# Routing tokens to experts for the second time: a shorter choice, roots between the scatters, and places and ranks in another order

## The reference

```python
x = _layernorm(x + attn(x))                      # softmax(q k^T) per batch, then v and Wo
x = _layernorm(x + expert_mlp(x, token_ids))     # expert = token_id // 3125, weights from ctx
x = _layernorm(x + ffn(x))                       # router, top 1 of 4 experts
# expert_mlp: silu(x Wg[e]^T) * (x Wu[e]^T), then Wd[e]^T; the weights are ctx_2048 (256 x 256 per expert)
# ffn: logits = x @ Wr + br; probs = softmax(logits); e = argmax; out = probs[e] * (silu(x Wg[e]) * (x Wu[e])) @ Wd[e]
```

## Time and profile before

| | us |
|---|---|
| runs, median of 3 | 197.58 (197.44 to 198.25) |
| span of the profiled execution | 194.3 |
| median above the span | 3.3 |
| PE busy | 176.0 (91%) |
| DVE, ACT, POOL busy | 132.0, 103.3, 103.0 |

### The profile page before, as it was taken

One profiled execution on the slowest core, in us unless ns is written; L12 is line 12 of the kernel. 1 busy time (PEld: TensorE's weight loads), 2 busy tenths in 40 slices (PEclk: granted clock), 3 DMA queues, 4 the chain that ended last, 5 costly groups with the idle time before them and its releaser, 6 DMA issues.

```text
span 194.3 us, 3905 instructions
## 1 busy us (share of the span) xinstructions
PE 176.0 (91%) x969; PEld 140.0 (72%) x969; DVE 132.0 (68%) x406; ACT 103.3 (53%) x274; POOL 103.0 (53%) x130
## 2 busy tenths in 40 slices
PE   1999997999999898989999999999999999999810
PEld 0677775447888655668888788888888888888610
DVE  3269996895678887536554454444799986888950
ACT  3136776725567935537664946643665422455530
POOL 7006356770126884627772168860588810377683
PEclk9999999999999999999999999999999999999975
DMA  5999999246999223146544105444050000011010
GB/s 157 359 336 418 378 366 319 73 139 168 322 334 405 101 85 94 29 130 173 221 149 150 46 0 165 164 162 167 0 162 3 0 0 3 0 57 56 22 62 24
DMA packets 15317, 29.14 MB, mean 150 GB/s; under 512 B 1726, under 2 KB 11968, under 8 KB 15170
## 3 DMA queue, kind: packets, MB, share of 16 engines
q1 hardware_dynamic: 13568, 25.68, 39.4%
q0 software_dynamic: 1440, 3.22, 4.7%
q10 hardware_dynamic: 290, 0.01, 0.1%
HBM read 20.41 MB, written 9.28 MB: 153 GB/s over the span
## 4 chain that ended last, share of the span: by engine, by line
PE 68%; POOL 11%; issue 7%; DMA 5%; DVE 3%; ACT 3%; POOLq 1%; SPq 1%; DVEq 0%; ACTq 0%
PE bank L484 14%; PE bank L486 13%; PE bank L485 13%; POOL out_tokens L473 5%; PE bank L729 4%; PE bank L563 4%; PE bank L652 3%; PE bank L629 3%; POOL rstd L395 3%; DMA arena<-in_attn_w 3%; PE bank L594 2%; PE bank L572 2%; PE bank L511 2%; DMA x_sorted<-buf,slot 1%; PE bank L498 1%
## 5 line engine op out<-in xcount | busy, mean ns | idle before, releaser
L391 POOL TENSOR_TENSOR w_lo<-stage,w_hi 128x512 fp32r<-128x512 f32 x40 | 51.4, 1305 | 44.0 <-ACT w_hi L803 44.0
L912 ACT ACTIVATE gate<-bank 128x256 f32<-128x256 f32 x44 | 17.0, 387 | 48.5 <-PE bank L486 48.5
L1206 DVE TENSOR_TENSOR hid<-bank,gate 128x256 f32<-128x256 f32 x44 | 18.7, 425 | 30.5 <-ACT gate L912 30.2
L484 PE MATMUL bank<-w_hi,xr 128*128 x88 | 35.9, 408 | 1.4 <-DVE xr L1164 0.8
L486 PE MATMUL bank<-w_hi,xr 128*128 x88 | 34.7, 395 | 0.0
L485 PE MATMUL bank<-w_lo,xr 128*128 x88 | 34.7, 394 | 0.0
L484 PE MATMUL bank<-w_hi,hT 128*128 x88 | 28.5, 324 | 0.7 <-DVE hT L1211 0.7
L803 ACT ACTIVATE w_hi<-stage 128x512 fp32r<-128x512 f32 x48 | 28.6, 630 | 0.3 <-PE bank L486 0.3
L486 PE MATMUL bank<-w_hi,hT 128*128 x88 | 24.9, 282 | 0.0
L485 PE MATMUL bank<-w_lo,hT 128*128 x88 | 24.8, 282 | 0.0
L484 PEld LDWEIGHTS bank<-w_hi,xr 128*128 128x128 f32 x88 | 16.6, 189 | 4.4 <-issue 2.3
(11 more groups left out here) (182 smaller groups left out, 329.7 us busy)
## 6 DMA issues: line engine op xcount, KB each, us to landing
stage<-in_w_ffn SPq DMA_DIRECT2D x16, 768.0 KB, 4.5
rows<-x_sorted SPq DMA_DIRECT2D x22, 132.0 KB, 2.3
x_sorted<-padrow SPq DMA_DIRECT2D x1, 2244.0 KB, 10.2
x_sorted<-padrow SPq DMA_DIRECT2D x1, 2112.0 KB, 16.4
buf<-in_x_tok SPq DMA_DIRECT2D x1, 1024.0 KB, 11.0
w_hi<-in_ctx SPq DMA_DIRECT2D x1, 1024.0 KB, 11.5
w_hi<-in_ctxT SPq DMA_DIRECT2D x1, 1024.0 KB, 14.0
x_sorted<-padrow SPq DMA_DIRECT2D x1, 792.0 KB, 12.7
```

What stands on the lines that cost most here:

```text
L391: g.tensor_tensor(out=lo, in0=src, in1=hi.bitcast(F32), op=ALU.subtract).then_inc(split_lo, 1)
L484: mm(dst, xhi, whi, start=start, stop=False)
L912: a(gate[:, (T + j) % 2, :], fA[j % 2][:, 0:FQ], ACT.Silu).then_inc(silu_done, 1)
L1206: v.tensor_tensor(out=hid[:, (T + j) % 2, :], in0=fA[j % 2][:, FQ:2 * FQ], in1=gate[:, (T + j) % 2, :], op=ALU.mult).then_inc(h_done, 1)
```

## The change

It touches the second sort and its surroundings, and nothing of the MLPs' products.

- **Choice.** `choose(n)` becomes: the norm's shift `nmr2` (formerly ACT's), one instruction per tile for the logits, a running maximum (scan) over the group, a comparison with the last element, and a difference of neighbours. An extra column carries the row's token number. Empty rows carry 2^126 there and tokens a negative number, so that an empty row chooses nothing. `validity()` becomes `move_tokens()` with two copies.
- **Roots.** The addition of epsilon moves from POOL to DVE, behind the moments; `root2` is one instruction. The roots are written into a column of `buf` and travel with the row.
- **POOL's order** puts roots 1, 2, 3 and 4 between scatters.
- **DVE's order.** `choose(n)` at i = 5, 7, 9 and `place(n)` at i = 6, 8, 10 stand directly behind `hidden(i)`, ahead of `residual(i-2)`; `choose(3)` stands ahead of `residual(10)`, and the early tables of weight offsets behind `place(3)`.
- **PE's order.** `rank(n)` for n = 0 to 2 stands behind the down products at i = 6, 8, 10; `rank(4)` behind `fup(0)`. Idle products: 6 before and 14 behind `rank(3)`, formerly 12 and 6.
- **ACT's order.** No `shift2`; the norms stand at other steps, the last two behind `fxhi(0)`.
- **Gates.** Logits and their maxima for the gate are made again from the sorted rows, `shifted_logits()`, in the third stage.

```diff
             def root2(n):
                 a, b = GROUPS[n]
-                pool.wait_ge(aggr2_ready, n + 1)
-                g.tensor_scalar(out=ve2[:, a:b], in0=mv2[:, a:b, 1], scalar1=EPS, scalar2=None,
-                                op0=ALU.add).then_inc(pool_step, 1)
-                pool.wait_ge(pool_step, n + 1)
+                pool.wait_ge(ve2_ready, n + 1)
                 g.tensor_tensor(out=rstd2[:, a:b], in0=ve2[:, a:b], in1=mhalf[:, a:b],
                                 op=ALU.pow).then_inc(rstd2_ready, 1)
...
-            validity()
+            move_tokens()
+            pool.wait_ge(tok_moved, 2)
             root2(0)
+            pool.wait_ge(d_init2, 32)
+            scatter2(0)
             root2(1)
-            pool.wait_ge(d_init2, 32)
-            for t in range(0, 3):
+            for t in range(1, 4):
                 scatter2(t)
             root2(2)
-            for t in range(3, ROUTED):
-                scatter2(t)
+            scatter2(4)
+            scatter2(5)
             root2(3)
+            scatter2(6)
             root2(4)
             for t in range(ROUTED, T):
                 scatter2(t)
...
+            RANK_AT = {GROUPS[n][1] + 3: n for n in range(3)}
...
-                if i == 7:
-                    rank(0)
-                if i == 9:
-                    rank(1)
                 if 2 <= i:
                     down(i - 2)
-                if i == 10:
-                    rank(2)
-            idle_products(12)
+                if i in RANK_AT:
+                    rank(RANK_AT[i])
+            idle_products(6)
             rank(3)
-            idle_products(6)
+            idle_products(14)
...
             ftx(0)
-            rank(4)
...
                     if i < len(items):
                         fup(i)
+                    if i == 0:
+                        rank(4)
...
-            SHIFT_AT = {6: 0, 9: 1, 10: 2}
-            NORMS_AT = {7: (0, 1), 8: (2,), 9: (3, 4), 10: (5, 6)}
+            NORM_BEFORE_SILU = {6: 0, 7: 2, 8: 3, 10: 5}
+            NORM_BEHIND_COPY = {6: 1, 8: 4, 10: 6}
...
-                last = v.bn_aggr(mv2[:, t, :], stats[:, t % 2, :])
+                step(v.bn_aggr(mv2[:, t, :], stats[:, t % 2, :]))
                 if t in GROUP_ENDING:
-                    last.then_inc(aggr2_ready, 1)
+                    s, e = GROUPS[GROUP_ENDING[t]]
+                    v.scalar_tensor_tensor(out=ve2[:, s:e], in0=mv2[:, s:e, 1], scalar=EPS, in1=ones_f[:, 0:e - s],
+                                           op0=ALU.add, op1=ALU.mult).then_inc(ve2_ready, 1)
...
             def choose(n):
...
                 dve.wait_ge(rstd2_ready, n + 1)
...
+                v.scalar_tensor_tensor(out=nmr2[:, a:b], in0=mv2[:, a:b, 0], scalar=-1.0, in1=rstd2[:, a:b],
+                                       op0=ALU.mult, op1=ALU.mult).then_inc(nmr2_ready, 1)
+                for t in range(a, b):
+                    v.scalar_tensor_tensor(out=choice[:, t, 1:E + 1], in0=buf[:, t, LOG:LOG + E], scalar=rstd2[:, t:t + 1],
+                                           in1=br_all[:], op0=ALU.mult, op1=ALU.add).then_inc(logit_ready, 1)
+                dve.wait_ge(logit_ready, b)
+                step(v.tensor_tensor_scan(out=run[:, a:b, :].rearrange("p t e -> p (t e)"),
+                                          data0=cap[:, 0:w, :].rearrange("p t e -> p (t e)"),
+                                          data1=choice[:, a:b, :].rearrange("p t e -> p (t e)"),
+                                          initial=LOW, op0=ALU.min, op1=ALU.max))
+                step(v.tensor_tensor(out=at_max[:, a:b, :], in0=run[:, a:b, :],
+                                     in1=run[:, a:b, E + 1:E + 2].broadcast_to([P, w, E + 2]), op=ALU.is_equal))
+                v.tensor_tensor(out=m2[:, a:b, :], in0=at_max[:, a:b, 1:E + 2], in1=at_max[:, a:b, 0:E + 1],
+                                op=ALU.subtract).then_inc(mask_ready, 1)
...
+            CHOOSE_AT = {GROUPS[n][1] + 2: n for n in range(3)}
+            PLACE_AT = {GROUPS[n][1] + 3: n for n in range(3)}
             for i in range(T):
                 hidden(i)
-                if i == 7:
-                    residual(5)
-                    choose(1)
...
+                if i in CHOOSE_AT:
+                    choose(CHOOSE_AT[i])
+                if i in PLACE_AT:
+                    place(PLACE_AT[i])
+                if i >= 2:
+                    residual(i - 2)
             early_tables()
             residual(9)
+            choose(3)
             residual(10)
-            choose(3)
             place(3)
+            offset_tables(0, EARLY)
             choose(4)
             fxlo(0)
             place(4)
```

More of the change, by code:

```diff
@@ L31 @@
 FAR = float(1 << 20)
-LOG, TOK, ROW = D, D + E, 264
+TOK0 = 1024
+TOK_SCALE = -2.0 ** 100
+NO_TOKEN = 2.0 ** 126
+LOW, HIGH = -3e38, 3e38
+LOG, TOK, RSTD, ROW = D, D + E, D + E + 1, 264
 XL = D + E
@@ L117, in route_kernel @@
         base8 = sb("base8", [P, T + 2, E + 1], BF16)
-        prio2 = sb("prio2", [P, T, E])
         pos2 = sb("pos2", [P, T, E + 1])
         slot2 = sb("slot2", [P, T], I32)
-        valid = sb("valid", [P, T])
-        nrs2 = sb("nrs2", [P, T])
+        cap = sb("cap", [P, 3, E + 2])
+        choice = sb("choice", [P, T, E + 2])
+        run = sb("run", [P, T, E + 2])
+        at_max = sb("at_max", [P, T, E + 2])
+        tok_abs = sb("tok_abs", [P, T])
         whole = sb("whole", [P, BLOCKS])
@@ L357, in _ @@
             const(g.memset(mhalf[:], -0.5))
-            const(g.memset(lw[:], 0.5))
+            const(g.memset(choice[:], LOW))
             const(g.memset(buf[:, :, LOG:ROW], 0.0))
@@ L864, in norm2 @@
             def norm2(t):
[L865 removed]
+                act.wait_ge(nmr2_ready, GROUP_OF[t] + 1)
                 a(buf[:, t, 0:D], buf[:, t, 0:D], ACT.Identity, bias=nmr2[:, t:t + 1],
                   scale=rstd2[:, t:t + 1]).then_inc(x2_ready, 1)
[L869 to L875 removed]
             def evict(t):
@@ L892, in _ @@
                     h1copy(i - 1)
-                if i in SHIFT_AT:
-                    shift2(SHIFT_AT[i])
-                for t in NORMS_AT.get(i, ()):
-                    norm2(t)
-            for t in ADDED_BY_PE:
-                evict(t)
-            for n in range(GROUP_OF[ROUTED], len(GROUPS)):
-                shift2(n)
-                for t in range(*GROUPS[n]):
-                    norm2(t)
+                if i in NORM_BEHIND_COPY:
+                    norm2(NORM_BEHIND_COPY[i])
+            evict(9)
+            evict(10)
+            norm2(7)
+            norm2(8)
             def fxhi(t):
@@ L947, in _ @@
                 if i == T:
-                    a(lexp[:], rows[:, :, LOG:LOG + E], ACT.Exp).then_inc(lexp_done, 1)
+                    act.wait_ge(lshift_ready, 1)
+                    a(lexp[:], lshift[:], ACT.Exp).then_inc(lexp_done, 1)
         @block.vector
@@ L1109, in choose @@
                 w = b - a
-                lm = buf[:, a:b, LOG:LOG + E]
                 if n == 0:
-                    dve.wait_ge(valid_ready, 1)
+                    dve.wait_ge(tok_moved, 1)
+                    dve.wait_ge(tok_ready, 2)
                 dve.wait_ge(rstd2_ready, n + 1)
-                step(v.tensor_tensor(out=logit[:, a:b, :], in0=lm,
-                                     in1=rstd2[:, a:b].unsqueeze(2).broadcast_to([P, w, E]), op=ALU.mult))
-                step(v.tensor_tensor(out=logit[:, a:b, :], in0=logit[:, a:b, :],
-                                     in1=br_all[:].unsqueeze(1).broadcast_to([P, w, E]), op=ALU.add))
@@ L1225, in fsum, with shifted_logits @@
                                                 in1=rows[:, t, 0:D], op0=ALU.mult, op1=ALU.add))
+            def shifted_logits():
+                step(v.tensor_tensor(out=logit[:], in0=rows[:, :, LOG:LOG + E],
+                                     in1=rows[:, :, RSTD:RSTD + 1].broadcast_to([P, T, E]), op=ALU.mult))
+                step(v.tensor_tensor(out=logit[:], in0=logit[:], in1=br_all[:].unsqueeze(1).broadcast_to([P, T, E]),
+                                     op=ALU.add))
+                step(v.tensor_reduce(out=lmax[:], in_=logit[:], axis=AX.X, op=ALU.max))
+                v.tensor_tensor(out=lshift[:], in0=logit[:],
+                                in1=lmax[:].unsqueeze(2).broadcast_to([P, T, E]), op=ALU.subtract).then_inc(lshift_ready, 1)
             def gates():
@@ L1230, in gates @@
                 step(v.reciprocal(topw[:], lsum[:]))
-                step(v.tensor_copy(outidx[:], rows[:, :, TOK]))
+                step(v.scalar_tensor_tensor(out=tok_abs[:], in0=rows[:, :, TOK], scalar=-1.0, in1=rows[:, :, TOK],
+                                            op0=ALU.mult, op1=ALU.max))
+                step(v.tensor_scalar(out=outidx[:], in0=tok_abs[:], scalar1=-1.0 / TOK_SCALE, scalar2=float(-TOK0),
+                                     op0=ALU.mult, op1=ALU.add))
             def finish(t):
```

79 lines of the change are left out of this document (28 added, 51 removed).

## The result

The changed kernel takes **202.73 us** (median of 4 runs, 202.57 to 203.03) against 197.51 (196.98 to 198.25) for the kernel before on the same chip: ratio 1.0300 [1.0252, 1.0349], 5.2 us slower. On a second chip it took 202.30 against 197.21 (experiment a0). Sign and mechanism are as forecast; the size was 4.0. As a number 202.73 lies inside the stated 198.8 to 203.3; carried to the 197.58 that the forecast started from, the ratio gives 203.5, just above it. One execution of the kernel before, on the chip of x1 to x5, took 618.61 us and is left out of the ratios.

What follows compares the result with a forecast made beforehand. TensorE was taken as the bound, through when it can start the third MLP and take its tile 3. A start 2.3 later plus 1.7 in PE's queue made 4.0: 197.6 + 4.0 = 201.6 us, range 198.8 to 203.3.

Steps and rivals of the forecast that it cites:

- The 6 + 14 idle products cost nothing: PE around rank 3: fourteen idle products end at 76.6, before the sorted rows at 77.0, so no cost.
- the clock left out of it: PE's granted clock was taken to stay at 1.00 despite forecast single idle times up to 1.3 us; nothing added.
- the token steps: Third stage, DVE: two small instructions replace one conversion at the same idle engine, at no cost.
- The loop of roots and scatters: Second sort: each group's root stands behind a scatter needing the previous group's places; scatter 6 at 72.1 instead of 69.67.
- The gap between scatters 8 and 9: Sign on POOL that the forecast is right: a gap of over 3 us there.
- PE's three waits: PE waits at rank 1, rank 2 and tile 10's transpose: about 3 us against 0.7, its stage ending about 1.4 later.
- the 3.3 that I took for what lies around the span: Median of 197.58 stands 3.3 above the profiled span of 194.3; the forecast difference was added to the median.
- Scatter 6, +2.4: First half of the second sort: scatter 6 starts at 72.1 instead of 69.67, making the early rows 2.4 us later.
- The second half, +1.7 behind the first product: Start of the third MLP: rank 4 behind the first product costs PE about 0.7 before `fup(1)` and 1.0 before `fth(0)`.
- Only the last rank costs: Rival: the sort keeps its pace, rank 4 puts scatter 10 at 80.2 against 78.81; 198.6 to 199.3; chance 0.19.
- The halves cancel: Rival: shorter choices (2 us of DVE) and earlier ranks make up for the waits; 197.6; chance 0.07.
- The clock falls too: Rival: PE falls to 1.2 GHz at the third MLP's start, one or two items slower; 204 to 206; chance 0.06.

Runs made afterwards that it cites:

- a0: The changed kernel unedited, run on another chip: 202.30 us, 1.0264 of the kernel before.
- x1: The changed kernel with POOL's scatters and roots back in the old order: 200.93 us, 1.0258 of the kernel before.
- x5: The changed kernel with five idle products in PE's 1.23 us wait before tile 10's transpose: 201.98 us, 1.0305 of the kernel before.
- x10: x8 with POOL's order of the change (roots between the scatters): 199.15 us, 1.0096 of the kernel before.
- x11: x8 with the last rank behind the first up product instead of ahead of it: 198.23 us, 1.0056 of the kernel before.
- y1: x8 with both POOL's order of the change and the last rank behind the first up product: 202.33 us, 1.0267 of the kernel before.
- x12: The changed kernel with idle products (3, 3 and 5) in PE's three waits before the third MLP: 200.82 us, 1.0186 of the kernel before.
- y2: The changed kernel with 6 instead of 14 idle products behind rank 3: 201.79 us, 1.0273 of the kernel before.
- x4: The changed kernel with the two token steps one MLP item earlier, away from POOL's weight splits: ratio 1.0291 to the kernel before.
- x8: All new instructions with every order, rank and the idle products of the kernel before, plus x4's edit: 195.21 us, 0.9959 of the kernel before.
- x6: The changed kernel with x1, x2 and x4 together, 6 idle products for 14, ScalarE's last two norms put back: 196.55 us, 1.003 of the kernel before.
- x2: The changed kernel with rank 4 back ahead of the first product: 201.34 us, 1.0265 of the kernel before.
- x7: The changed kernel with nearly all padding (32 of 33 blocks) in the first of its two transfers: 207.87 us, 1.0604 of the kernel before.

## Why the mechanism was right, and which terms of the sum failed

**The failed step, in short.** The sum went wrong in two terms that it put at nothing, "The 6 + 14 idle products cost nothing" together with the clock left out of it, and the token steps. The runs showed 1.1 us for the first and 0.8 to 1.0 us for the second. The loop of roots and scatters itself was mis-sized by 0.5 (scatter 6 +2.9 for +2.4).

**Right.** The main steps of the mechanism are in the trace. Root 1 ends at 61.57 (forecast 61.3). Choice 1 waits for POOL, 1.46 (1.8), choice 2 1.01 (1.0). Scatter 6 starts at 72.60 (72.1). Scatter 10 follows the first product by 4.25 (4.2). The gap between scatters 8 and 9 is 3.76 (over 3). PE's three waits are 2.60 together (about 3), though the 1.23 among them stays when the roots are moved back (x1). The MLP keeps its pace from tile 3 on, but for the token steps. x10 and x11 show each of the two causes alone, y1 that they suffice.

**Wrong in size: +4.0 forecast, +6.8 in the span and +5.2 in the medians.** The two measures differ mostly because the profiled execution of before was some 1.4 quicker than its median; the 3.3 that I took for what lies around the span had this in it. The steps below are those of the profiles, in order:

- *Scatter 6, +2.4.* It was +2.9. A choice took 1.11 (61.60 to 62.71), not 0.95: the two logits took 0.41 together, not 0.08 each. The bound of 1.4 held; the middle was too low.
- *"The 6 + 14 idle products cost nothing."* This failed. Rank 3 came at 75.55 instead of 73.5, the fourteen ended with the first transpose at 78.64, and the rows had needed until about 77.5 (72.60 and the usual 4.9). 1.1 us. Here the forecast had also added PE's waits wrongly: 3 us against 0.7 make its stage end 2.3 later, and I had booked 1.4. At full clock (x5, x12, y2, counted from scatter 0) it is 2.5, in the changed kernel 4.2. I had written down the cover, idle products over at 76.6 and rows at 77.0, and not that 0.4 of slack is less than the error of either number.
- *The clock, left out of the sum and given 0.06 at the MLP's start.* The fall came earlier, in tile 9's and tile 10's down products, at 1.72 and 1.66 instead of 1.04. That is 1.3 us on PE, and most of what made rank 3 late (1.4 of the 2.05, by the counts from scatter 0), so this item and the one before are one chain. Without the fall rank 3 would come at about 74.2 and the fourteen idle products end near 77.5, just when the rows are there (an estimate from x12's distances): they cost the 1.1 only because the clock fell ahead of them. My evidence for leaving it out, a stretch with one wait of 0.58 at 3.33 busy of 4, didn't cover PE at 2.14 of 4. Price: 1.5 us by x12's median, 1.0 to 1.2 at tile 3. The latter is the 1.1 of the item above, seen from its cause, and is not added again.
- *The second half, +1.7 behind the first product.* It was +2.0 (11.17 from the first product to tile 3's, against 9.16 before).
- *The token steps "replace one conversion by two small instructions at the same idle engine".* This failed: that place isn't idle on POOL. The conversion of before had waited in the same way, as DVE's timeline of the kernel before shows, in a row that I had not looked at:

```profile
111.42 0.66 DVE L1231 CAST outidx<-rows 128x11 int32<-128x11 f32 x1
```

  1.0 us by x4, 0.8 against before.

0.5 + 1.1 + 0.1 (rows to first product) + 0.3 make tile 3 later by 2.0 than forecast, and the tokens add 0.8: 6.8, the difference of the two spans. Against it stands the quick execution of before, so that 5.2 remain in the medians.

**The rivals.** "Only the last rank costs" was half of it: by x11 that alone is 2.0 us by the ratio (1.0056 against 0.9956) and 2.4 by the distance to tile 3, more than the 1.0 to 1.7 that I gave it. I had counted scatter 10 and not what stands behind the places on DVE. "The halves cancel" rested on the shorter choices; these are real (x8 with x4's edit is 0.4% faster than before), but the new order spends them many times over. "The clock falls too" was true together with the forecast, not instead of it: I had made two parts of one chain into alternatives.

**Open.** Why x6 (1.003), with only the new orders of DVE, ScalarE and the early ranks left, and 6 for 12 idle products ahead of rank 3, stands 0.7% above x8 was not split further; its profile shows PE waiting 1.23 us for tile 10's hidden product and 0.89 for the mask of rank 3. And as said, which executions fall to half clock.

## What to carry to other kernels

Before a producer is moved behind a consumer on an in-order queue, ask what that consumer waits for. Here a root needed by the next choice stood behind a scatter that needed the choice before: a loop over three engines that paid a wait in every turn, while its parts were cheaper than the old ones. Undo such changes together as well as singly: x1 and x2 each looked worthless, because each left the other's wait (and the late idle products) as the next bound. And new instructions and new orders are to be timed apart; here the instructions with x4's edit gained 0.4% and the two orders cost 3%.

## What the hardware showed that I had not expected

- **The clock fell without a long pause.** PE's single waits before the fall were 0.74, 0.63 and 1.23 us, with 2.14 us of 66 to 70 busy, and the clock was at 0.50 from 71 to 74 although PE was then busy throughout. With 2.13 (y2) and 2.74 (x1) of 4 it stayed at 1.00 in other executions. Counted from scatter 0, the fall cost 1.0 to 1.2 us at tile 3. The Trainium skill ("TensorE: Matmul & The Clock Gate", "A second HAM failure mode: psum-queue depth-cycling") tells of a kernel whose clock swings because PE goes idle briefly and often between groups of products; the trace agrees in so far as the clock fell behind short waits; it fell once here and did not swing.
- **Small DVE instructions waited for a POOL elementwise operation.** 0.17 us became 0.67 and 1.21 beside splits of 1.27 each, and each ended within 0.05 us of a split's end. The Trainium skill ("GPSIMD Engine Reference", "Key points") says that the two engines share their way to SBUF and get in each other's way for some forms of DVE's instructions; the trace agrees, and the second instruction lasted nearly as long as the split beside it. x4, which moves them away from the splits, gives back the 0.17. The other small steps beside these two (0.19 and 0.23) were not held.
- **A transfer of padding is not free for being early.** 4224 KB at once took 23.6 us to land and moved the whole second stage by 5 us (x7); the 2244 KB of the kernel before landed in 10.2.
